# Thirteen expert tiles inside the mixer steps: a fused Mamba mixer and mixture-of-experts layer on one core

## The chip, the cores and the metric

The kernel runs on one core of one Trainium2 chip. The metric is device microseconds of one launch. Before the change the median of three runs is 4983.12 us (4978.73 to 4983.15).

## The reference, cut to what matters

All tensors are float32. There are 4096 tokens (8 sequences of 512) of width 512.

```
x  = x + mamba(layernorm(x))        # in_proj 512 -> 2*1024, causal conv of 4 taps, silu,
                                    # x_proj 1024 -> 128 + 16 + 16, dt_proj 128 -> 1024,
                                    # softplus, scan over time with 16 states per channel,
                                    # y * silu(z), out_proj 1024 -> 512
x  = x + moe(layernorm(x))          # 8 experts, top 2 of 8, weights renormalised
# one expert on its rows:  (silu(r @ w1[e]) * (r @ w3[e])) @ w2[e]     512 -> 1792 -> 512
```

The scan is `h = h * exp(delta*A) + delta*x*B_t` and `y_t = sum_n h*C_t`. The experts see the rows of layernorm(x) after the mixer; each token's row goes to two experts, and each expert's result, times its routing weight, is added to the output.

## The kernel before, in words

There are two programs in one launch, one after the other.

**The mixer** (`mixer`) works off 256 tokens (T) in each of 16 steps (STEPS). The emission of step s holds three strands at once: the scan of tokens s (`scan`), the front of tokens s+1 (`front`: transposes, x and z products, convolution, dt, softplus), and the back of tokens s-1 (`back`: output product, residual, second norm, routing, scattering rows to the expert buffer `rows_d`). A step is cut into 16 slots (SLOTS, index u) and each slot into two pieces (32 pieces; a piece is 4 states of one chunk of 128 channels). The order on every engine is written out by hand: `beside(u)` on TensorE and ScalarE and `beside(u, g)` on VectorE say what is done beside the scan in slot u. Per piece

- ScalarE computes four decays `dA` (L468, `decays`), which is allowed once piece k-3 has been scanned;
- VectorE multiplies the inflow `pU` (L869) and scans `hs` (L886), which waits for the decay and for `summed` of piece k-4 (there are NB = 4 buffers);
- GpSimd multiplies `hs` by C (L399, `weigh`) and, in pieces 1 to 12, does one convolution sum (L422);
- TensorE sums over the states by transposes that accumulate (L747, `sums`).

Beside them TensorE does the x products in slots 0 to 3 and the z products in slots 13 to 15 and in slot 0 of the next step (all L624), the output product in slots 3 to 6 (L671), the x_proj products in slots 9 and 10 (L681, L686), the dt products in slots 11 and 12 (L706), the transposes and router logits in slots 10 and 11 (L715, L694), ranks in slot 14 (L724). VectorE adds the residual in slots 5 and 7 (L904, `residual`), after which the second norm and `route` follow in small operations. At the end of a step VectorE does the softplus (L986, L992, L995) and GpSimd issues four indirect DMAs that scatter the rows (L383, `scatter`).

SyncE issues all other DMAs in one fixed order: four loads of `win` of 1 MB a step (L289), `xb`, `xf`, the store of the output rows, and at the end of the step the four broadcast loads of B and C into `bc` (L338, 1 MB each), each held until its old contents have been used. `each_step` unrolls steps -1, 0 and the last four and runs the rest in a hardware loop of 6 turns with 2 steps in each.

**The expert program** (`experts`) starts when the mixer has ended. VectorE works out how many 128-row tiles each expert has; then each tile t takes its rows, transposes them (L1279), makes up and gate products (L1292, 112 products of 128 columns), silu (L1250), and the down product (L1301, 14 products of 512 columns), and GpSimd adds the rows to the output by an indirect DMA (L1165). The weights of one expert are resident and are loaded only where the expert changes. With these inputs there are 67 tiles.

Of the kernel before, what the change touches and what calls it, by code (L numbers as in the profile page):

```python
# [19 lines left out]
F32 = mybir.dt.float32  # L20
# [5 lines left out]
P = 128  # L26
# [26 lines left out]
NT = 2 * TOKENS // P + E - 1  # L53
NT_SURE = 2 * TOKENS // P
# [4 lines left out]
MK = M // P  # L59
LN1P_SMALL = 1.0 / 128  # L60
# [12 lines left out]
def mixer(nc, x, w_in, conv_w, w_x, w_dt, dt_bias, a_log, d_par, w_out, gate, out, rows_d, bc_d, cnt_d):  # L73
    with ExitStack() as ctx:
# [8 lines left out]
        win = [sb(f"win{s}", [P, DC, 4 * P]) for s in range(2)]  # L83
# [13 lines left out]
        xb = sb("xb", [P, TT, D])  # L97
        rows = [sb(f"rows{k}", [P, TT, RW]) for k in range(2)]
# [16 lines left out]
        x2T = sb("x2T", [P, DC, T])  # L115
# [25 lines left out]
        pM = [pb(f"pM{s}", [P, 2, T]) for s in range(2)]  # L141
# [20 lines left out]
        pT = pS[:, :].rearrange("p (d q) -> p d q", d=DC)  # L162
        pR = pS[:, 0:2 * (TT + 1) * E].rearrange("p (a t e) -> p a t e", a=2, t=TT + 1)
# [13 lines left out]
        win_in = [sem(f"win_in{s}") for s in range(2)]  # L177
# [48 lines left out]
        second_rows = sem("second_rows")  # L226
# [11 lines left out]

        pool_turn = sem("pool_turn")
# [4 lines left out]
        NSET = 12 + NB  # L244
# [7 lines left out]
        def each_step(eng, emit):  # L252


            for s in (-1, 0):
                emit(s, s % 2)
            with eng.Fori(0, (STEPS - 4) // 2) as i:
                emit(2 * i + 1, 1)
                emit(2 * i + 2, 0)
            for s in range(STEPS - 3, STEPS + 1):  # L260
                emit(s, s % 2)
# [3 lines left out]
        def has(s):  # L265

            if not isinstance(s, int):
                return True, True, True, True
            return 0 <= s < STEPS, s + 1 < STEPS, s + 2 < STEPS, s >= 1

# [3 lines left out]
        def _(sp):  # L274
# [9 lines left out]
            def step(s, odd):  # L284
                scan, front, ln1, back = has(s)
                f, r = s + 1, s - 1

                def load_win(j):
                    sp.dma_start(win[j % 2][:, :, :], w_in[:, :, j * 4 * P:(j + 1) * 4 * P]).then_inc(win_in[j % 2], 16)  # L289

                def load_weights():
# [5 lines left out]
                    sp.dma_start(out[TOKENS:TOKENS + P, :], x2T[:, 0:D // T, :]).then_inc(weights_in, 16)  # L297

                if front:

                    hold(z_mm, PAIRS * s + 2)
                    load_win(0)
                if back:
                    hold(x1_stored, 16 * r)
                    hold(xn2, TT * r)
                    sp.dma_start(xb[:, :, :], tokens(x, r)).then_inc(xb_in, 16)
                if front:
                    hold(z_mm, PAIRS * s + 4)
                    load_win(1)
                if isinstance(s, int) and s < 0:  # L310
                    load_weights()
                if ln1:
# [3 lines left out]
                if front:  # L316
                    hold(x_mm, PAIRS * f + 2)
                    load_win(2)
                    hold(x_mm, PAIRS * f + 4)
                    load_win(3)  # L320
                if back:
                    hold(x1_ready, TT * r + TT)
                    sp.dma_start(tokens(out, r), xb[:, :, :]).then_inc(x1_stored, 16)
                if front:
# [4 lines left out]
                    sp.dma_start(bc_d, bcs[:, :]).then_inc(bc_stored, 16)  # L329
                    hold(bc_stored, 16 * f + 16)  # L330
# [15 lines left out]
            sp.dma_start(cnt_d, ebase[0:1, :]).then_inc(cnt_stored, 16)  # L346
            sp.wait_ge(cnt_stored, 16)
# [5 lines left out]
        def _(pool):  # L353
            pool.memset(x2T[:, 0:D // T, :], 0.0).then_inc(consts_set, 1)
# [5 lines left out]
            for i, v in enumerate((LN1P_SHIFT, LN1P_SMALL, EPS)):  # L360
# [14 lines left out]
                      allow_small_or_imprecise_dtypes=True).then_inc(consts_set, 1)  # L375
            def scatter(n, k, t):
# [1062 lines left out]
```

## Time and profile before

| | |
|---|---|
| median of 3 runs | 4983.12 us |
| time of the profiled execution | 4978.98 us |
| span of its trace, first to last instruction | 4977.2 us |
| mean granted TensorE clock | 0.917 |
| busy: PE, DVE, ACT, POOL | 4293.8, 2425.1, 1883.4, 1703.3 us |

The span and the profiled execution's time are 1.8 us apart, so sums made on the trace can be set against the times directly. PE is TensorE, PEld its weight load, DVE VectorE, ACT ScalarE, POOL GpSimd, SP SyncE. A float32 product shows as two instructions. The busy time of PE counts time at either clock, so that the same work shows as more busy time where the clock was low.

### The profile page before, as it was taken

What the parts mean: (1) busy time and instruction counts of PE and PEld (TensorE: products, weight loads), DVE (VectorE), ACT (ScalarE), POOL (GpSimd) and SP (SyncE); (2) the same over time, 40 slices, a digit from 0 to 9 for tenths busy, and PEclk for the clock granted to TensorE, in tenths of its full rate; (3) what the DMA queues carried; (4) which work ended last, traced back from release to release, by engine and by line L of the source; (5) the groups of instructions that cost most, each with busy time, mean ns of one, the idle gap of its engine ahead of it and who ended that gap; (6) DMA issues with size and microseconds to landing.
All of it is one profiled execution on the core that took longest, in us unless ns stands there. A gap on an engine that the chain in (4) does not pass through costs nothing.

```text
span 4977.2 us, 73101 instructions
## 1 busy us (share of the span) xinstructions
PE 4293.8 (86%) x25764; PEld 3442.3 (69%) x25764; DVE 2425.1 (49%) x3184; ACT 1883.4 (38%) x3876; POOL 1703.3 (34%) x1215
## 2 busy tenths in 40 slices
PE   6677777777777777775599999999999999999999
PEld 4556555655656566554488888888878878878877
DVE  3999999999999999999200000000000000000000
ACT  6777777777777777765000000000000000000000
POOL 3667676666767667675100000000000000000000
PEclk8888888888888888886799999999999999999999
DMA  3121122222112222210300303003031030120300
GB/s 141 71 70 55 68 90 90 85 82 74 53 67 90 90 85 81 77 60 17 133 15 15 101 14 104 13 13 105 13 101 17 13 101 17 51 63 17 101 13 15
DMA packets 132824, 308.67 MB, mean 62 GB/s; under 512 B 8596, under 2 KB 17428, under 8 KB 124308
## 3 DMA queue, kind: packets, MB, share of 16 engines
q1 hardware_dynamic: 116564, 269.55, 15.6%
q0 software_dynamic: 14768, 34.41, 3.7%
q10 hardware_dynamic: 1296, 2.37, 0.1%
q8 instruction: 89, 1.46, 0.1%
q14 instruction: 107, 0.88, 0.1%
HBM read 920.96 MB, written 45.95 MB: 194 GB/s over the span
## 4 chain that ended last, share of the span: by engine, by line
PE 51%; ACTq 0%; DMA 0%; issue 0%; POOL 0%; DVE 0%; ACT 0%; SPq 0%; POOLq 0%; DVEq 0%
PE pA L1292 17%; PE pB L1292 17%; PE pD L1301 16%; PE pX L1279 1%; DMA rows_d<-pad 0%; ACTq L1260 0%; ACTq L1261 0%; DMA xr<-rows_d 0%; POOL out L1165 0%; ACTq L1259 0%; POOL tnum L1153 0%; DVE ow L1386 0%; ACT xT L1263 0%; POOL pad L1146 0%; SPq L1182 0%
## 5 line engine op out<-in xcount | busy, mean ns | idle before, releaser
L399 POOL TENSOR_TENSOR hs<-hs,bc 128x1024 f32<-128x1024 f32 x512 | 1213.1, 2369 | 404.1 <-DVE hs L886 382.7
L886 DVE TENSOR_TENSOR_SCAN hs<-dA,pU 128x1024 f32<-128x1024 f32 x512 | 1168.5, 2282 | 22.9 <-DVE pU L869 2.1
L747 PE MATMUL pY<-ident,hs 128*128 128x128 f32 x4096 | 647.2, 314 | 464.4 <-POOL hs L399 464.3
L1250 ACT ACTIVATE gate<-pA 128x512 f32<-128x512 f32 (+1 forms) x268 | 145.7, 544 | 2311.1 <-PE pB L1292 2311.1
L1292 PE MATMUL pA<-xT,w1s 128*128 128x128 f32 x7504 | 992.7, 275 | 0.7 <-ACT xT L1263 0.7
L1292 PE MATMUL pB<-xT,w3s 128*128 128x128 f32 x7504 | 992.0, 275 | 0.0
L747 PEld LDWEIGHTS pY<-ident,hs 128*128 128x128 f32 x4096 | 543.6, 162 | 587.1 <-POOL hs L399 510.7
L1292 PEld LDWEIGHTS pA<-xT,w1s 128*128 128x128 f32 x7504 | 920.0, 192 | 32.7 <-issue 31.6
L1165 POOL DMA_INDIRECT out<-ow,trow x67 | 104.6, 1561 | 2437.7 <-DVE ow L1386 2401.0
L1292 PEld LDWEIGHTS pB<-xT,w3s 128*128 128x128 f32 x7504 | 914.2, 192 | 0.0
L468 ACT ACTIVATE dA<-delta,aneg 128x255 f32<-128x255 f32 x2048 | 849.5, 507 | 149.9 <-DVE hs L886 136.0
L1301 PE MATMUL pD<-w2s,hT 128*128 128x512 f32 x1876 | 816.2, 592 | 0.0
L1382 DVE TENSOR_TENSOR hT<-gate,pB 128x512 f32<-128x512 f32 (+1 forms) x268 | 166.5, 621 | 1111.9 <-ACT gate L1250 1111.6
L869 DVE TENSOR_TENSOR pU<-pZ,bc 128x1024 f32<-128x1024 f32 x512 | 629.5, 1230 | 29.6
L1301 PEld LDWEIGHTS pD<-w2s,hT 128*128 128x128 f32 x1876 | 351.2, 190 | 416.6 <-issue 416.6
L624 PE MATMUL pM<-xnT,win 128*128 128x256 f32 x2048 | 518.9, 413 | 4.9 <-ACT uv L531 3.1
L624 PEld LDWEIGHTS pM<-xnT,win 128*128 128x128 f32 x2048 | 427.8, 214 | 70.3 <-ACT uv L531 3.5
L1386 DVE TENSOR_SCALAR ow<-pD,wrow 128x512 f32<-128x512 f32 x67 | 50.3, 751 | 784.7 <-PE pD L1301 784.7
L671 PE MATMUL pS<-wout,sz 128*128 128x512 f32 x512 | 249.2, 633 | 1.4 <-issue 0.9
L422 POOL TENSOR_TENSOR xc<-xc,uv 128x512 f32<-128x512 f32 x192 | 227.0, 1182 | 13.3 <-POOL uv L416 6.1
L1377 DVE CAST trow<-xr 128x1 int32<-128x1 f32 x67 | 10.3, 154 | 405.4 <-DMA out<-ow,trow 388.0
L671 PEld LDWEIGHTS pS<-wout,sz 128*128 128x128 f32 x512 | 102.6, 209 | 107.6 <-issue 106.0
(168 smaller groups left out, 2568.4 us busy)
## 6 DMA issues: line engine op xcount, KB each, us to landing
w1s<-in_w SPq DMA_DIRECT2D x204, 1024.0 KB
w3s<-in_w SPq DMA_DIRECT2D x204, 1024.0 KB
w2s<-in_w SPq DMA_DIRECT2D x204, 1024.0 KB
win<-in_w_in SPq DMA_DIRECT2D x64, 1024.0 KB, 5.3
bc<-bc_d SPq DMA_DIRECT2D x64, 1024.0 KB, 4.8
w1s<-in_w SPq DMA_DIRECT2D x68, 512.0 KB
w3s<-in_w SPq DMA_DIRECT2D x68, 512.0 KB
w2s<-in_w SPq DMA_DIRECT2D x68, 512.0 KB
```

Of the source, the lines that this page charges most:

```text
L399: pool.tensor_tensor(hs[b][:, :, :], hs[b][:, :, :], bc[:, N + g * PN:N + (g + 1) * PN, :], ALU.mult)\
L422: pool.tensor_tensor(xcf[:, 2 * pair:2 * pair + 2, :], xcf[:, 2 * pair:2 * pair + 2, :], y[:, 2 * k:2 * k + 2, k:k + T], ALU.add).then_inc ...
L468: e = act.activation(dA[k % NB][:, i, 1:T], delta[:, c, 1:T], ACT.Exp, scale=aneg[:, c, n:n + 1])
L624: m = pe.matmul(ps[:, h, :], win[j % 2][:, d, wcol:wcol + P], rowsT[:, d, :], start=d == 0, stop=d == DC - 1)
L671: m = pe.matmul(pO[:, :], szr[:, c, t * P:(t + 1) * P], wout[:, c, :], start=c == 0, stop=c == CH - 1)
L747: m = pe.matmul(pY[c % 2][:, t * P:(t + 1) * P], hs[k % NB][:, i, t * P:(t + 1) * P], ident[:, :], start=g == 0 and i == 0 and t == 0, sto ...
L869: dve.tensor_tensor(pU[:, :, :], pDx[:, :].rearrange("p (a t) -> p a t", a=1).to_broadcast([P, PN, T]), bc[:, g * PN:(g + 1) * PN, :], ALU ...
L886: dve.tensor_tensor_scan(hs[b][:, :, :].rearrange("p n t -> p (n t)"), dA[b][:, :, :].rearrange("p n t -> p (n t)"), pU[:, :, :].rearrange ...
L1250: act.activation(gate[q % 2][:, 0:n, :], pA[q % 2][:, 0:n, :], ACT.Silu).then_inc(silu, 1)
L1292: m = pe.matmul(ps[q % 2][:, k, :], ws[:, d, cols], xT[:, d, :], start=d == 0, stop=d == DC - 1)
L1301: m = pe.matmul(pO[:, :], hT[:, k, :], w2s[:, k, :], start=k == 0, stop=k == MK - 1)
L1382: dve.tensor_tensor(hT[:, lo:lo + n, :], gate[q % 2][:, 0:n, :], pB[q % 2][:, 0:n, :], ALU.mult)\
```

## The change: what it does, and the diff

One full tile of 128 rows of one expert is worked off in each of the mixer steps 3 to 15 (13 tiles). At the end of the step before, VectorE picks the expert with the most rows not yet worked off (`pick`, 8 operations on one partition). In the step SyncE loads the rows, and the expert's 11 MB of weights through a ring of three buffers `ew` of 512 KB, in 21 loads. TensorE transposes the rows in slot 2, makes 16 products of 128 columns in each of slots 4 to 10 and the 14 down products of 512 columns in slots 11 to 15, all into one PSUM bank `pE`. ScalarE takes tanh(g/2) of each up round, VectorE makes `(tanh + 1) * g` and `* 0.5 * up` from it. In the next step, after piece 2, GpSimd adds the rows to the output. The expert program takes 13 tiles fewer and starts at each expert's next row. To make room for `pE` the two banks `pM0` and `pM1` become one, with the x products alternating between it and `pS`, and the z and dt products all in `pM`; `win` becomes three buffers of 512 KB. The rows to be scattered are normalised in place in `xb`, so the second set waits until the first has been written. `each_step` unrolls steps -1 to 3 and the last three, and loops 5 times over 2 steps.

```diff
-NT = 2 * TOKENS // P + E - 1
-NT_SURE = 2 * TOKENS // P
+EARLY0 = -(-(E * (P - 1) + 1) // (2 * T)) + 1      # 3
+EARLY = STEPS - EARLY0                              # 13
+NT_SURE = 2 * TOKENS // P - EARLY
+NT = NT_SURE + E - 1
+PK = 2
+ROUNDS = MK // PK                                   # 7
+EW = 3
+EWLOADS = 3 * ROUNDS                                # 21
-        win = [sb(f"win{s}", [P, DC, 4 * P]) for s in range(2)]
+        win = [sb(f"win{s}", [P, DC, 2 * P]) for s in range(3)]
+        ew = [sb(f"ew{i}", [P, 2 * D]) for i in range(EW)]
-        pM = [pb(f"pM{s}", [P, 2, T]) for s in range(2)]
+        pM = pb("pM", [P, 2, T])
+        pE = pb("pE", [P, 512])
+        pX = [pS[:, :].rearrange("p (h t) -> p h t", h=2), pM]
+        UP0, DOWN = 4, {11: (0, 4), 12: (4, 8), 13: (8, 10), 14: (10, 12), 15: (12, 14)}
# SyncE, order within one step
+                if tile:
+                    hold(e_next, jt + 1)
+                    expert = sp.value_load(epick_i[0:1, 0:1], min_val=0, max_val=E - 1)
+                    row = sp.value_load(epick_i[0:1, 1:2], min_val=0, max_val=DUMMY - P)
+                    for i in range(EW):
+                        load_expert(i)          # each held until load i-3 has been used
...
+                if tile:
+                    hold(ew_used, EWLOADS * jt + 2 * ROUNDS)      # xf comes after up round 7
+                    sp.dma_start(xf[:, :, :], tokens(x, s + 2)).then_inc(xf_in, 16)
...
+                    hold(z_mm, PAIRS * f + 3)
+                    load_win(0, 1)
+                if front:
                     hold(bc_stored, 16 * f + 16)
                     for g in range(UPC):                          # the four bc loads
# GpSimd
+                if k == 1 and t == 0:
+                    ge(pool, scattered, 16 * TT * (2 * n + 1))
+                    pool.tensor_copy(xb[:, :, WCOL], w_second[:, :]).then_inc(second_w, 1)
+                    if i == 2 and early(s)[1]:
+                        add_rows(s - 1 - EARLY0, s - 1)
# ScalarE
+                def read_dt(q):
+                    ge(act, dt_mm, 4 * f + q + 1)
+                    for h in range(2):
+                        ...                     # Abs and Identity of pM[:, h, :]
+                    if tile and UP0 <= u < UP0 + ROUNDS:
+                        ge(act, ew_used, EWLOADS * jt + 2 * (u - UP0) + 2)
+                        ge(act, e_h, ROUNDS * jt + u - UP0)
+                        act.activation(eth[:, :, :], pEup[:, 0, :, :], ACT.Tanh, scale=0.5).then_inc(e_tanh, 1)
# TensorE
+                def expert(u):
+                    if UP0 <= u < UP0 + ROUNDS:
+                        j = u - UP0
+                        ge(pe, e_h, ROUNDS * jt + j)
+                        for w in range(2):
+                            i = 2 * j + w
+                            ge(pe, ew_in[i % EW], 16 * (EWLOADS // EW * jt + i // EW + 1))
+                            for k in range(PK):
+                                for d in range(DC):
+                                    m = pe.matmul(pEup[:, w, k, :], part[:, d, k * P:(k + 1) * P], exT[:, d, :], ...)
+                            m.then_inc(ew_used, 1)
+                    if u in DOWN:
+                        for k in range(*DOWN[u]):
+                            m = pe.matmul(pE[:, :], ehT[:, k, :], ew[i % EW][:, k % PK * D:(k % PK + 1) * D], ...)
# VectorE, slot u, after the first scan of the slot (g == 1)
+                    j = u - UP0 - 1
+                    if 0 <= j < ROUNDS and g == 1:
+                        ge(dve, e_tanh, ROUNDS * jt + j + 1)
+                        dve.scalar_tensor_tensor(eth, eth, 1.0, pEup[:, 0], ALU.add, ALU.mult).then_inc(e_half, 1)
+                        ge(dve, e_half, ROUNDS * jt + j + 1)
+                        dve.scalar_tensor_tensor(ehT[:, PK * j:PK * (j + 1), :], eth, 0.5, pEup[:, 1],
+                                                 ALU.mult, ALU.mult).then_inc(e_h, 1)
```

## Rows read from the trace of the kernel before

**Rows 1.** The page: busy time and share of the span, then tenths in 40 slices

```profile
PE 4293.8 (86%) x25764; PEld 3442.3 (69%) x25764; DVE 2425.1 (49%) x3184; ACT 1883.4 (38%) x3876; POOL 1703.3 (34%) x1215
...
PE   6677777777777777775599999999999999999999
...
DVE  3999999999999999999200000000000000000000
...
PEclk8888888888888888886799999999999999999999
```

**Rows 2.** Windows of mixer and expert program: start:end, length, busy by engine, clock

```profile
400.00:2220.00 1820.00, 1383.33 (x6773) 1068.97 (x6772) 1719.52 (x2102) 1324.19 (x2771) 1257.19 (x891) 0.85 0.21 74
2640.00:4900.00 2260.00, 2260.00 (x15443) 1856.00 (x15442) 208.03 (x424) 166.86 (x301) 95.13 (x61) 1.00 0.18 48
```

**Rows 3.** Chain that ended last, 2790 to 2870 us: start, length, what

```profile
2794.85 0.89 PE pB L1292 x8
...
2819.41 12.02 PE pD L1301 x28
...
2856.88 12.02 PE pD L1301 x28
```

**Rows 4.** Line 593, once a step: count, duration in ns, first and last start

```profile
L593 ACT ACTIVATE delta<-uv,ones x16: 2002/2005/2012, 78.8 to 2228.2; 128x2048 f32<-128x2048 f32 x16
```

**Rows 5.** Groups of VectorE, 400 to 2220 us: busy, mean ns, idle before

```profile
L886 DVE TENSOR_TENSOR_SCAN hs<-dA,pU 128x1024 f32<-128x1024 f32 x406 | 926.5, 2282 | 17.4 <-DVE pU L869 1.9 <-DVE pU L876 1.8
...
L986 DVE SCALAR_TENSOR_TENSOR uv<-dA,uv 128x1024 f32<-128x1024 f32 x24 | 50.1, 2124 | 0.0
L897 DVE TENSOR_TENSOR sz<-pY,sz 128x256 f32<-128x256 f32 x102 | 42.7, 418 | 0.1
...
L904 DVE TENSOR_TENSOR xb<-pS,xb 128x512 f32<-128x512 f32 x26 | 18.0, 691 | 23.9 <-PE pS L671 23.9
...
L848 DVE TENSOR_TENSOR head<-delta,aneg 128x128 f32<-128x128 f32 x6 | 1.8, 292 | 22.6 <-issue 22.6
```

**Rows 6.** Timeline of VectorE, one step: start, length, operation, idle before

```profile
934.35 2.29 DVE L886 TENSOR_TENSOR_SCAN hs<-dA,pU 128x1024 f32<-128x1024 f32 x1
...
946.63 1.23 DVE L869 TENSOR_TENSOR pU<-pZ,bc 128x1024 f32<-128x1024 f32 x1
...
989.39 0.69 DVE L904 TENSOR_TENSOR xb<-pS,xb 128x512 f32<-128x512 f32 x1 [2.10 <-PE pS L671]
```

**Rows 7.** Timeline of TensorE, 930 to 1045 us

```profile
934.77 2.32 PE L624 MATMUL pM<-xnT,win 128*128 128x256 f32 x10
...
980.50 3.60 PE L671 MATMUL pS<-wout,sz 128*128 128x512 f32 x8
983.93 1.91 PE L747 MATMUL pY<-ident,hs 128*128 128x128 f32 x16
...
1012.49 1.97 PE L747 MATMUL pY<-ident,hs 128*128 128x128 f32 x8 [2.96 <-POOL hs L399]
```

**Rows 8.** Timeline of GpSimd at the start of that step

```profile
949.97 0.96 POOL L383 DMA_INDIRECT rows_d<-rows,idx  x1 [0.30 <-issue]
950.93 0.20 POOL L396 COPY state<-hs 128x4 f32<-128x4 f32 x1
```

**Rows 9.** Timeline of SyncE's queue, then DMA issues: count, KB each, us to landing

```profile
925.46 14.03 SPq L336 DMA_DIRECT2D bc<-bc_d  x4
...
win<-in_w_in SPq DMA_DIRECT2D x49, 1024.0 KB, 5.3
bc<-bc_d SPq DMA_DIRECT2D x49, 1024.0 KB, 4.7
...
out<-ow,trow POOLq DMA_INDIRECT x61, 4.8
```

**Rows 10.** Groups of ScalarE, 400 to 2220 us: two of its table loads, one tap copy

```profile
L505 ACT ACTIVATE uv<-pM,convw 128x256 f32<-128x256 f32 x294 | 117.8, 483 | 0.0
...
L593 ACT ACT_TABLE_LOAD x12 | 15.4, 1283 | 0.2
L600 ACT ACT_TABLE_LOAD x12 | 15.4, 1283 | 0.2
```

More of the change, by code:

```diff
@@ L96, in mixer @@
         xf = sb("xf", [P, TT, D])
-        xb = sb("xb", [P, TT, D])
-        rows = [sb(f"rows{k}", [P, TT, RW]) for k in range(2)]
+        xb = sb("xb", [P, TT, RW])
         xnT = [sb(f"xnT{s}", [P, DC, T]) for s in range(2)]
@@ L176, in mixer @@
         xn1 = sem("xn1")
-        win_in = [sem(f"win_in{s}") for s in range(2)]
+        win_in = [sem(f"win_in{s}") for s in range(3)]
         turned1 = sem("turned1")
@@ L237, in mixer @@
         tok_set = sem("tok_set")
+        e_next = sem("e_next")
+        e_step = sem("e_step")
+        e_rows = sem("e_rows")
+        e_meta = sem("e_meta")
+        ew_in = [sem(f"ew_in{i}") for i in range(EW)]
+        ew_used = sem("ew_used")
+        e_turned = sem("e_turned")
+        e_xT = sem("e_xT")
+        e_tanh = sem("e_tanh")
+        e_half = sem("e_half")
+        e_h = sem("e_h")
+        e_tok = sem("e_tok")
+        e_ow = sem("e_ow")
+        e_added = sem("e_added")
         pool_turn = sem("pool_turn")
@@ L285, in step, with load_win @@
                 scan, front, ln1, back = has(s)
+                tile = early(s)[0]
                 f, r = s + 1, s - 1
-                def load_win(j):
-                    sp.dma_start(win[j % 2][:, :, :], w_in[:, :, j * 4 * P:(j + 1) * 4 * P]).then_inc(win_in[j % 2], 16)
+                jt = s - EARLY0
+                def load_win(z, pair):
+                    slot, col = (WIN_Z if z else WIN_X)[pair], (PAIRS * z + pair) * 2 * P
+                    sp.dma_start(win[slot][:, :, :], w_in[:, :, col:col + 2 * P]).then_inc(win_in[slot], 16)
                 def load_weights():
@@ L314, in step @@
+                if back:
+                    hold(scattered, 16 * 2 * TT * r)
+                    hold(x1_stored, 16 * r)
+                    sp.dma_start(xb[:, :, 0:D], tokens(x, r)).then_inc(xb_in, 16)
+                if front:
+                    hold(x_mm, PAIRS * f + 3)
+                    load_win(1, 3)
+                    hold(x_mm, PAIRS * f + 4)
+                    load_win(1, 1)
+                if ln1 and not tile:
                     hold(turned1, TT * f + TT)
                     sp.dma_start(xf[:, :, :], tokens(x, s + 2)).then_inc(xf_in, 16)
[L316 to L320, printed above, removed]
+                if tile:
+                    for i in range(EW, 9):
+                        load_expert(i)
@@ L321, in step @@
                 if back:
                     hold(x1_ready, TT * r + TT)
-                    sp.dma_start(tokens(out, r), xb[:, :, :]).then_inc(x1_stored, 16)
+                    sp.dma_start(tokens(out, r), xb[:, :, 0:D]).then_inc(x1_stored, 16)
+                if tile:
+                    for i in range(9, 14):
+                        load_expert(i)
                 if front:
@@ L436, in _ @@
             pool.wait_ge(scattered, 16 * 2 * TT * STEPS)
+            pool.wait_ge(e_added, 16 * EARLY)
         @block.scalar
@@ L572, in step @@
                         decays(u + 1)
+                    else:
+                        halfway(u)
                     if u < SLOTS - 1:
@@ L618, in step, with dt @@
                 f, r = s + 1, s - 1
+                tile, jt = early(s)[0], s - EARLY0
                 xcf, szr = xc[1 - odd], sz[1 - odd]
-                def project(ps, rowsT, wcol, j, h):
+                def dt(q):
+                    if q == 0:
+                        ge(pe, dtr_copied, f + 1)
+                    else:
+                        ge(pe, dt_read, 4 * f + q)
+                    for h in range(2):
+                        c = 2 * q + h
+                        m = pe.matmul(pM[:, h, :], wdt[:, c * P:(c + 1) * P], dtr[:, :], start=True, stop=True)
+                    m.then_inc(dt_mm, 1)
@@ L697, in beside @@
                     if u in (11, 12) and front:
[L698 to L707 removed]
+                        dt(2 * (u - 11))
                     if u == 10 and back:
@@ L718, in beside @@
                         z_pair(u - 13, f, xnT[1 - odd])
+                    if tile:
+                        expert(u)
                     if u == 14 and back:
@@ L835, in step @@
                 f, r, fodd = s + 1, s - 1, 1 - odd
+                (tile, _, picks), jt = early(s), s - EARLY0
                 xcs, xcf = xc[odd], xc[1 - odd]
@@ L1001, in beside @@
                     c = u // UPC
+                    if tile:
+                        expert(u, g)
                     if scan and u % UPC == 0 and c >= 2 and g == 0:
```

335 lines of the change are left out of this document (243 added, 92 removed).

## The prediction

> **What bounds the kernel now.** I read the page first. Its slices show two programs end to end [rows 1]: in the first 18 or so VectorE is at nine tenths and TensorE at seven, in the last 20 TensorE is at nine and all else is near nothing. The windows give the sizes [rows 2]. From 2640 to 4900 us TensorE is busy for 2260 of 2260 us at a granted clock of 1.00, so the expert program is TensorE's alone. From 400 to 2220 us VectorE is busy 1719.5 of 1820 us (94%), ScalarE 73%, GpSimd 69%, TensorE 1383.3 us (76%) at a mean clock of 0.85.
>
> The chain of waits gives the price of a tile: the 28 down instructions start at 2819.41 and again at 2856.88, so 37.47 us, of which 12.02 are the down products and the rest up products of 0.89 us per 8 instructions [rows 3]. The Ln of the softplus (L593) runs once a step, 16 times from 78.8 to 2228.2 us: a step lasts 2149.4 / 15 = 143.3 us [rows 4].
>
> Why a step lasts 143 us: the scan (2.28 us) runs 32 times, and almost nothing else ends VectorE's idle time. The named waits in the 1820 us are 23.9 us for TensorE's output product (L904) and 22.6 us of "issue" before L848, the first operation of the loop body, 4.5 us at each of five back edges [rows 5]. So VectorE sets the mixer, TensorE the experts, and each has the other engine partly free.
>
> **The change part by part, against the profiled span of 4977 us (4979 us for that execution, 4 us under the median of 4983).**
>
> *Removed.* 13 tiles of the expert program: 13 x 37.47 = 487 us. All of it is on the path, since TensorE never rests there. Nothing is late in its place: the rows and weights of a tile come in beside it as before.
>
> *Added, TensorE.* A tile in the mixer is the same products, at full clock the same 37.5 us. Room for it: 1383.3 us in 1820 is 108.9 us per step at a clock of 0.85, which is 92.6 us of work at full clock, an estimate. Eight transposes after a rest of 2.96 us take 1.97 us, sixteen without a rest 1.91 us [rows 7]: the first at the level of 1.2 GHz, the second at 2.4. With fewer rests most of the step should run at 2.4 GHz. 92.6 + 37.5 = 130 us then stand in a step of 143. It fits on average, with about 10 us lost at each boundary between steps where TensorE waits for VectorE and ScalarE; it doesn't fit in every slot.
>
> *Added, VectorE, direct.* Two scalar_tensor_tensor of 128x256 in each of 7 rounds, reading PSUM and SBUF. The nearest row is L897, same form, 0.42 us [rows 5]; back to back its pitch is a little less, and the second waits for the first: 0.80 us a round, 5.6 us a step. Bounds: 0.33 x 2 x 7 = 4.6 us (pitch alone), and a quarter of L986 (2.12 us for 1024 columns [rows 5]), 0.53 x 2 x 7 = 7.4 us. Eight picks and one copy of the token number at 0.1 to 0.15 us: 1.1 us. Sum **6.7 us** a step, all of it on VectorE's path.
>
> *Added, waits of VectorE for TensorE in slots 4 to 7.* A round is TensorE, then tanh, then VectorE in the next slot after its first scan. TensorE's slot 4 holds 3.6 us of output product, 1.9 of sums, 0.7 of turning y, [rows 7] and now 3.6 us of up products: 9.7 us, against a VectorE slot of two pieces of 3.7 us plus a feed and the new 0.8, about 8.9. Slots 5 and 6 are alike; 7 and 8 have nothing else and catch up. VectorE waits for TensorE there already (2.10 us before the residual [rows 6]). Behind the waiting round on VectorE stands the next scan. I take 5 us a step; nothing if TensorE's better clock pays for it, and at most 3 x 3.6 + 2.1 = 13 us.
>
> GpSimd belongs to the same sum. The second pair of scatters now waits until the first pair has landed; the nearest landing is 4.8 us for an indirect store [rows 9]. GpSimd goes straight from its last scatter at 949.97 to the first piece at 950.93 [rows 8], so its pieces start some 5 us later, plus about 1.5 us for the added row store after piece 2. It has 3.95 us of work per piece while it convolves, against VectorE's 3.8, so the delay isn't won back before slot 6, and the sums and the output product come later. The four buffers (15 us) cover the scan, not the residual: 2 of the 5 us are this. In the three steps without a tile it costs 2 us each, **6 us** in all.
>
> *Added, slots 10 and 11.* TensorE has the dtr product (3.6 us), two transposes with ScalarE between them, and the up round: about 11 us. VectorE meets that tanh after its first scan in slot 11. The dt products now go through one bank in four quarters, each behind ScalarE's reading of the one before. I take 2.5 us; from 0 to 7 us (each of three more exchanges with ScalarE at 2 us of reading).
>
> *Added, the end of the step.* The four bc loads move on SyncE behind the wait for the z product of slot 15 and behind a win load. Before, the first was issued at 925.46 [rows 9]; that z product (10 instructions at the start of the window shown) ends at 937.1 [rows 7]. Issue at about 938.5, one 512 KB load ahead (half of 5.3 us), 4.7 us to landing [rows 9]: 945.8, and VectorE's next pU stands at 946.63 [rows 6]. A cover of 20 us shrinks to 1. Whenever TensorE is late in slot 15, the scan is late too: 1.8 us; from 0 to 8 us (four loads of 4.7 us against 10 us of softplus).
>
> *Hidden.* The 21 weight loads: a load is issued when the buffer three back has been used, about a slot (9 us) before its use, and half of win's 5.3 us is 2.7 us. Bounds 0 and, at the full 5.3 us each, still 0. The late xf load (after up round 7, needed in slot 13) has more than a slot. ScalarE: seven tanh at about the 0.48 us of L505 [rows 10], two copies, less one copy of the rows: +3.5 us in an engine that rests for a quarter; nothing.
>
> The Trainium skill ("ScalarE: Activation LUTs", section "Table sets: the hidden batching unit") puts tanh with exp in one set, which would spare the loads; but it also says that ln then exp need one load, and the trace has one before each (L593 and L600, 1.28 us [rows 10]). By it tanh is free, and my sum agrees; since its other line isn't borne out here, the case where it fails stands below with a chance.
>
> The skill ("DMA: Bandwidth & Descriptors", section "Bandwidth") also wants 1 MiB or more per DMA for three quarters of peak, and the change halves that size. No row here shows 1 KB runs; if it doubled the transfer time, 5.3 us would still be under a slot and the sum would stay.
>
> *The ends.* The last scatter is on the path into the expert program: +5 us. One back edge fewer, 4 instead of 5: -4.5 us.
>
> **Sum.** A tile step grows by 6.7 + 5 + 2.5 + 1.8 = 16 us; 13 x 16 = 208. 4979 - 487 + 208 + 6 + 5 - 4.5 = 4706.5. I say **4705 us**. In general the time is 4498.5 + 13 g for a growth of g us per tile step; the change breaks even at g = 37.
>
> **The rivals.**
>
> A. *VectorE's own operations are all that shows*: g between 6.7 and 12, say 8, **4602 us**. For it: 13 us of room on TensorE, and a better clock. Against it: VectorE already waits for the output product, and the tight slots lie together.
>
> B. *TensorE becomes the bound.* The clock doesn't rise, since waits on tanh and on the products of VectorE make new rests in each round: 108.9 + 37.5/0.85 = 153 us, plus 10 us at the boundary, is 163: g = 20. With the bc loads late as well (5 us), g = 25: **4823 us**. For it: rests under 3 us already leave the clock at the lower level [rows 7]. Against it: nine slots will have hardly a rest.
>
> C. *Tanh and exp don't share a table.* Two loads of 1.28 us in each of 7 rounds are 18 us more on ScalarE in a step of which it rests 38; half exposed, g = 25, **4823 us**; bounds 4705 and 4705 + 13 x 18 = 4939.
>
> D. *Slower.* The round is a ring of three engines: TensorE can't start round j+1 before VectorE's product of round j, VectorE waits for tanh, and the sums that free the scan's buffers are queued on TensorE behind the products. If TensorE's work isn't beside the scan at all but between two scans, all 37.5 us and the 6.7 of VectorE stand in the step: g = 44, 4498.5 + 13 x 44.2 = **5073 us**. It decides from g = 37, when more than 30 of the 37.5 us are exposed. For it: the scan may run only four pieces ahead. Against it: four pieces are 15 us, more than any one slot adds.
>
> **How the numbers follow.** Forecast (g from 12 to 20: 4655 to 4759) 0.50; A 0.18 (4586 to 4655); B 0.22 (4759 to 4860); C 0.05; D 0.04; something that undoes nearly all the gain to within 0.2%, which is about what a measurement of this kernel tells from no change, 0.01. The range takes the forecast, most of A and the nearer half of B: **4615 to 4810 us**. Faster 0.95, same 0.01, slower 0.04.
>
> **What would show it.** The chain still goes through L1292 and L1301's lines, with 54 tiles of 37.47 us. The Ln of the softplus should come every 159 us in the tile steps and every 145 in the others. The granted clock of the mixer rises to 0.93 or more. VectorE's idle time names the tanh and the residual at 3 to 8 us a step, most of it in slots 5 to 7 and 11, and pU at the start of a step waits for bc by 1 to 3 us. No table load before tanh (a third group of loads beside it would be C). If tile steps stay under 155 us, the waits were overrated; above 163 us with a clock under 0.9 it is B; if TensorE waits for `ew`, the cover that I gave the ring was wrong.

## The result, and the profile after

The changed kernel takes 4790.66 us (median of 4 runs, 4779.15 to 4794.46) against 4981.69 us of the kernel before in the same comparison: ratio 0.9613, 95% interval 0.9601 to 0.9625. It is 191 us faster. The forecast was 4705 us, 277 us faster; the range of 4615 to 4810 us holds the time. The profiled execution took 4794.05 us, its span 4792.3 us.

The page, the same lines as [rows 1]:

```profile
PE 4208.5 (88%) x25764; PEld 3403.0 (71%) x25764; DVE 2471.3 (52%) x3377; ACT 1872.3 (39%) x3912; POOL 1706.9 (36%) x1233
...
PE   5777888888887988888887499999999999999999
...
DVE  3999988888888888888889300000000000000000
...
PEclk8788989989999989999898699999999999999999
```

VectorE has fallen from nine tenths to eight in the slices of the tile steps, although it has more to do; TensorE and its clock have risen. The expert program has 54 tiles. Its chain (the same view as [rows 3]) still shows down products 37.46 us apart:

```profile
2820.61 12.02 PE pD L1565 x28
...
2858.07 12.02 PE pD L1565 x28
```

So the 487 us taken away are as forecast; the span is 184.9 us shorter (4977.2 to 4792.3), so the mixer and its end gave back 302. The Ln of the softplus (now L752) places them. From its fourth start to its last there are 12 steps, in the trace before from 495.2 to 2228.2 us, now from 505.9 to 2513.6: 144.4 us became 167.3. The view of L752, as [rows 4]:

```profile
L752 ACT ACTIVATE delta<-uv,ones x16: 2002/2006/2010, 83.7 to 2513.6; 128x2048 f32<-128x2048 f32 x16
```

12 x 22.9 = 275 us. The other 27 us are 10.7 before that fourth start and 16.6 behind the last one, where the thirteenth tile stands in a step without a front.

A window of tile steps, the same view as [rows 2] (start:end, length, busy of PE, PEld, DVE, ACT, POOL, then clock, share of the DMA engines, GB/s):

```profile
500.00:2500.00 2000.00, 1673.13 (x9485) 1346.66 (x9484) 1719.64 (x2270) 1289.21 (x2733) 1213.70 (x861) 0.92 0.42 136
```

Per step of 167.3 us VectorE is busy 143.9 us and idle 23.5; per step of 144.4 us it was busy 136.4 and idle 8.0. Of 22.9 us of growth 7.4 are operations and 15.5 are waits. VectorE's waits in the 2000 us, which hold 12 steps (engine, line, releaser: us in total, times, longest):

```profile
DVE eth L1213 <- ACT eth L713: 84.7, 47, 5.5
...
DVE y L988 <- ACT sd L679: 35.3, 12, 3.4
DVE xb L1107 <- PE pS L877: 33.3, 12, 4.2
DVE pZ L1145 <- ACT le L701: 30.8, 12, 4.1
DVE pZ L1046 <- issue: 26.2, 4, 6.7
...
DVE pZ L1167 <- PE pS L924: 14.8, 11, 1.7
...
DVE hs L1089 <- ACT dA L629: 7.7, 8, 3.2
```

The tanh takes 7.1 us a step. The residual has gone from 1.9 (23.9 us in 12.6 steps, [rows 5]) to 2.8. The square root of the second norm (2.9), the router's exp (2.6) and the ranks (1.2) are new: VectorE hardly ever waited for them in the windows before.

How one step comes by these waits is seen on three timelines (start, length, operation, idle before). VectorE:

```profile
1403.04 0.69 DVE L1107 TENSOR_TENSOR xb<-pS,xb 128x512 f32<-128x512 f32 x1 [3.85 <-PE pS L877]
...
1438.54 0.17 DVE L988 RECIPROCAL y<-sd 128x2 f32<-128x2 f32 x1 [3.35 <-ACT sd L679]
...
1456.92 0.42 DVE L1213 SCALAR_TENSOR_TENSOR eth<-eth,pE 128x256 f32<-128x256 f32 x1 [2.51 <-ACT eth L713]
...
1468.95 0.42 DVE L1213 SCALAR_TENSOR_TENSOR eth<-eth,pE 128x256 f32<-128x256 f32 x1 [3.92 <-ACT eth L713]
```

ScalarE:

```profile
1424.85 0.39 ACT L713 ACTIVATE eth<-pE 128x256 f32<-128x256 f32 x1 [5.19 <-PE pE L810]
...
1430.11 1.91 ACT L671 ACTIVATE xc<-xc 128x2048 f32<-128x2048 f32 x1
...
1433.61 3.29 ACT L629 ACTIVATE dA<-delta,aneg 128x255 f32<-128x255 f32 x8
...
1438.22 0.29 ACT L679 ACTIVATE sd<-mv,series 128x2 f32<-128x2 f32 x1
```

TensorE:

```profile
1448.24 4.37 PE L887 MATMUL pM<-xc,wx 128*32 128x256 f32 x16
1452.55 3.84 PE L810 MATMUL pE<-xf,ew 128*128 128x128 f32 x32
...
1457.97 3.62 PE L893 MATMUL pM<-xc,wx 128*128 128x256 f32 x16
```

ScalarE stands 5.19 us for the up products before a tanh. Decays, the silu of the convolution with a table load on each side of it (L671), and the next decays are queued behind that tanh and ahead of the square root, which therefore starts only at 1438.22; VectorE, in slot 8, waits 3.35 us for it. In slot 9 TensorE does the B and C product first (4.37 us) and only then the up products, and VectorE waits 2.51 us for their tanh. In slot 10 the dt-rank product (3.62 us) and two transposes stand ahead of the up products, and the wait is 3.92 us. Added up by slot over the 12 steps, the tanh waits are 16.8 us in slots 5 to 7, nothing in 8 and 9, 18.1 in slot 10 and 49.8 in slot 11.

The wait for the router's exp comes about otherwise. The same step on TensorE, ScalarE and VectorE:

```profile
1481.33 3.60 PE L819 MATMUL pE<-ew,ehT 128*128 128x512 f32 x8
...
1486.76 0.47 ACT L603 ACTIVATE uv<-pM,dtb 128x256 f32<-128x256 f32 x1 [1.84 <-PE pM L789]
...
1488.36 1.91 ACT L698 ACTIVATE uv<-uv 128x2048 f32<-128x2048 f32 x1
...
1490.40 0.18 DVE L1145 TENSOR_REDUCE pZ<-le 128x2 f32<-128x16 f32 x1 [3.02 <-ACT le L701]
```

Four down products (L819) stand ahead of the last quarter of the dt product. ScalarE waits for that quarter, then takes the softplus's exp over 2048 columns (L698), and the router's small exp is queued behind it.

TensorE has time enough in the step as a whole (busy 140.0 us of 167.3); what VectorE stands for is the place of the work in TensorE's and ScalarE's queues.

### The profile page after: what moved, and what is told of

The parts are those of the page before. It is cut to its first block and busy times, and to the rows that moved or that the text cites. A ratio compares the mean times of both kernels' runs of the same rounds, so it can differ in the third digit from the quotient of the medians.

```text
span 4792.3 us, 73789 instructions
## 1 busy us (share of the span) xinstructions
PE 4208.5 (88%) x25764; PEld 3403.0 (71%) x25764; DVE 2471.3 (52%) x3377; ACT 1872.3 (39%) x3912; POOL 1706.9 (36%) x1233
## 3 DMA queue, kind: packets, MB, share of 16 engines
q1 hardware_dynamic: 273078, 412.71, 26.2%
## 5 line engine op out<-in xcount | busy, mean ns | idle before, releaser
L1514 ACT ACTIVATE gate<-pA 128x512 f32<-128x512 f32 x216 | 117.4, 544 | 1861.0 <-PE pB L1556 1861.0
L1556 PE MATMUL pA<-xT,w1s 128*128 128x128 f32 x6048 | 800.6, 275 | 0.7 <-ACT xT L1527 0.7
L1556 PE MATMUL pB<-xT,w3s 128*128 128x128 f32 x6048 | 799.9, 275 | 0.0
L1556 PEld LDWEIGHTS pA<-xT,w1s 128*128 128x128 f32 x6048 | 741.8, 192 | 26.4 <-issue 25.3
L1556 PEld LDWEIGHTS pB<-xT,w3s 128*128 128x128 f32 x6048 | 737.3, 192 | 0.0
L1565 PE MATMUL pD<-w2s,hT 128*128 128x512 f32 x1512 | 657.8, 592 | 0.0
L1072 DVE TENSOR_TENSOR pU<-pZ,bc 128x1024 f32<-128x1024 f32 x512 | 629.0, 1228 | 22.6
L1647 DVE TENSOR_TENSOR hT<-gate,pB 128x512 f32<-128x512 f32 x216 | 134.1, 621 | 898.8 <-ACT gate L1514 898.7
L827 PE MATMUL pM<-xnT,win 128*128 128x256 f32 x1536 | 404.4, 423 | 3.0 <-ACT uv L604 1.7
L810 PEld LDWEIGHTS pE<-xf,ew 128*128 128x128 f32 x2912 | 350.7, 199 | 45.7 <-issue 23.6
L810 PE MATMUL pE<-xf,ew 128*128 128x128 f32 x2912 | 357.6, 283 | 18.8 <-DVE ehT L1218 18.6
```

The source lines that it names most:

```text
L810: m = pe.matmul(pEup[:, w, k, :], part[:, d, k * P:(k + 1) * P], exT[:, d, :], start=d == 0, stop=d == DC - 1)
L827: m = pe.matmul(ps[:, h, :], w[:, d, h * P:(h + 1) * P], rowsT[:, d, :], start=d == 0, stop=d == DC - 1)
L1072: dve.tensor_tensor(pU[:, :, :], pDx[:, :].rearrange("p (a t) -> p a t", a=1).to_broadcast([P, PN, T]), bc[:, g * PN:(g + 1) * PN, :], ALU ...
L1556: m = pe.matmul(ps[q % 2][:, k, :], ws[:, d, cols], xT[:, d, :], start=d == 0, stop=d == DC - 1)
L1565: m = pe.matmul(pO[:, :], hT[:, k, :], w2s[:, k, :], start=k == 0, stop=k == MK - 1)
L1647: dve.tensor_tensor(hT[:, lo:lo + n, :], gate[q % 2][:, 0:n, :], pB[q % 2][:, 0:n, :], ALU.mult)\
```

## Experiments

Each ratio is against the kernel before, run on the same chip beside it (4981 to 4983 us).

**1. The rearrangement alone.** No tile in the mixer.

```diff
-EARLY = STEPS - EARLY0
+EARLY = 0
...
-            return EARLY0 <= s < STEPS, EARLY0 <= s - 1 < STEPS, EARLY0 <= s + 1 < STEPS
+            return False, False, False
-            sp.wait_ge(e_next, EARLY)
-            pool.wait_ge(e_added, 16 * EARLY)
```

> All of the rearrangement (one dt and z bank, three smaller win buffers, the scatter in two halves, the bc loads behind the z product, the later unrolling), but no tile in the mixer: all 67 tiles stay in the expert program. Theory W (the growth of a tile step comes from the tile itself, from waits between TensorE, ScalarE and VectorE): the three steps without a tile grew by 1.9 us each between the traces, so 16 steps give +30 us, less one loop jump of 5 us: about 5007 us, and a step of 145.5 us. Rival R (the rearrangement is what costs, each step 6 us or more): 5075 us or more. If it comes out at 4980 the rearrangement is free and my 6 us for it were too much.

Measured: 5021.03 us, ratio 1.0078 (1.0061 to 1.0094); 146.8 us a step. The rearrangement costs 40 us, 2.4 us a step, more than theory W's 30 and far less than R. Its VectorE waits from 840 to 2180 us:

```profile
DVE xb L1103 <- PE pS L873: 23.7, 13, 3.9
DVE pZ L1042 <- issue: 16.4, 4, 4.3
DVE hs L1085 <- ACT dA L625: 13.2, 9, 2.2
```

The scan's wait for decays was absent before and is 1.4 us a step here. It stands near the x products, not at the dt quarters: eight of the nine come 40 to 46 us behind the Ln. Before the decays of one of them ScalarE had waited for an x product in the one bank:

```profile
982.73 0.47 ACT L660 ACTIVATE xc<-pM,convw 128x256 f32<-128x256 f32 x1 [4.83 <-PE pM L823]
```

In this window ScalarE waits 66.3 us in all for x products in that bank; before the change it waited 32.0 us for x products (L503) in the same window. Whether the one bank is what makes them late wasn't tried. A tile costs 167.3 - 146.8 = 20.5 us on top.

**2. Fewer up products.** Only a quarter of the inputs is multiplied, so 28 products in place of 112; everything else stays.

```diff
-                                for d in range(DC):
-                                    m = pe.matmul(pEup[:, w, k, :], part[:, d, ...], exT[:, d, :],
-                                                  start=d == 0, stop=d == DC - 1)
+                                m = pe.matmul(pEup[:, w, k, :], part[:, 0, ...], exT[:, 0, :], start=True, stop=True)
```

> Leaves out three of four up products of each mixer tile (only the first 128 of the 512 inputs are used), so TensorE has 28 products in place of 112 per tile, 18.7 us less per tile step; loads, tanh, VectorE's products and all waits stay. Theory W1 (TensorE's time stands in VectorE's way through the tanh): the waits of 7.1 (tanh), 2.8 (residual), 2.9 (square root) and 2.6 us (exp of the router) per tile step go nearly all, so 10 to 15 us of the 24 go: 4791 - 13 x 13 = about 4620 us. Rival W2 (the chain of hand-overs costs, not TensorE's time): 4740 to 4790 us.

Measured: 4674.85 us, 0.9382 (0.9366 to 0.9398); 157.5 us a step. That is between W1 (4620) and W2 (4740 to 4790), somewhat nearer W1. 18.7 us less of TensorE bring 9.8 us a step by the traces and 8.9 by the medians. Of VectorE's waits from 500 to 2350 us (11.7 steps) these two matter:

```profile
DVE pZ L1144 <- ACT le L701: 29.8, 11, 3.0
...
DVE eth L1212 <- ACT eth L713: 7.2, 9, 1.2
```

The tanh wait has fallen from 7.1 to 0.6 us a step and the square root's is gone. The router's exp still costs 2.5 us: it isn't the up products that hold it, which agrees with the timeline above.

**3. VectorE's products later.** The products of a round come one scan later; the down products move too, since the last round is ready later.

```diff
-                    if 0 <= j < ROUNDS and g == 1:
+                    if 0 <= j < ROUNDS and g == 3:
-        UP0, DOWN = 4, {11: (0, 4), 12: (4, 8), 13: (8, 10), 14: (10, 12), 15: (12, 14)}
+        UP0, DOWN = 4, {12: (0, 4), 13: (4, 8), 14: (8, 10), 15: (10, 14)}
```

> VectorE makes the two products of a round after the second scan of the slot instead of the first (3.7 us later), and the down products stand in slots 12 to 15 (4, 4, 2, 4) instead of 11 to 15, so that the last product need not be there in slot 11. Theory W1: the tanh is then ready when VectorE comes, the wait of 7.1 us per tile step goes and little comes back, since TensorE's next round isn't due before: 4791 - 13 x 6 = about 4713 us. Rival W3 (TensorE is the bound in these slots, so that VectorE's wait only moves to the residual, the square root or the scan's buffers): 4770 to 4800 us.

Measured: 4861.99 us, 0.9761 (0.9745 to 0.9777); 172.0 us a step. My expectation fell, and beyond the rival too: 71 us slower than the changed kernel. VectorE's waits from 500 to 2350 us, then one tanh on ScalarE and the square root that VectorE waits for behind it:

```profile
DVE y L988 <- ACT sd L679: 80.7, 11, 8.5
DVE eth L1213 <- ACT eth L713: 51.1, 18, 5.2
```

```profile
1286.48 0.39 ACT L713 ACTIVATE eth<-pE 128x256 f32<-128x256 f32 x1 [3.42 <-PE pE L810]
...
1293.11 0.17 DVE L988 RECIPROCAL y<-sd 128x2 f32<-128x2 f32 x1 [8.00 <-ACT sd L679]
```

The tanh wait went down to 4.8 us a step (10.8 steps), but the square root's rose from 2.9 to 7.5. TensorE may not start a round before VectorE's product of the last one. With that product later the round and its tanh are later (ScalarE waits 3.42 us here), and the decays and the square root are queued behind the tanh. The ring is closed: what one engine gives up, another waits for.

**4. The second scatter pair later.**

```diff
                 for i in range(PIECES):
                     if scan:
                         weigh(s, odd, i)
+                    if i == 0 and (not isinstance(s, int) or s >= 2):
+                        for t in range(TT):
+                            scatter(s - 2, 1, t)
...
-                    for k in range(2):
+                    for k in range(2 if isinstance(s, int) and s == STEPS else 1):
```

> The second pair of scatters is issued after the first piece of the next step, so GpSimd doesn't stand for the first pair to land (80.4 us in 12 steps, 6.7 us a step). Theory P (GpSimd's late start is part of the residual wait and of the later waits): GpSimd starts its first piece 3 to 5 us earlier, the residual wait of 2.8 us goes, 2 to 3 us a step in 16 steps: about 4750 us. Rival: the four buffers cover the delay and nothing changes, 4785 to 4795 us. If the issue of two scatters between the first pieces is worse than the wait, it is slower: 4810 us.

Measured: 4788.9 us, 0.9611 (0.9595 to 0.9627): no change. GpSimd's wait for the first pair (80.4 us in 12 steps of the changed kernel) is gone from the trace, VectorE's waits are about as before (residual 2.7 and tanh 7.3 us a step), and the time is the same.

**5. Small weight loads.** The first tile's loads are whole, all later ones 8 KB, so the later tiles multiply by old weights.

```diff
+                    if not (isinstance(s, int) and s == EARLY0):
+                        sp.dma_start(ew[i % EW][:, 0:16], w1[bass.ds(expert * D, P), 0:16]).then_inc(ew_in[i % EW], 16)
-                    if i < 2 * ROUNDS:
+                    elif i < 2 * ROUNDS:
```

> After the first mixer tile each of the 21 weight loads moves 8 KB (16 columns of one chunk) instead of 512 KB, so the tiles work on old weights; all instructions and waits stay. In the trace of the changed kernel the bc loads land after 12.3 us (4.7 before) and the first scatters after 7.4 us. Theory W (engines wait for each other, not for transfers): 4785 to 4795 us, as the changed kernel. Rival M (the 10 MB a step crowd the other transfers, and that is part of the growth): 3 us or more per tile step, 4750 us or less.

Measured: 4780.44 us, 0.9598 (0.9582 to 0.9614), overlapping the changed kernel's interval. The DMA issues of both, first the changed kernel (count, KB, us to landing):

```profile
ew<-in_w SPq DMA_DIRECT2D x250, 512.0 KB, 4.4
bc<-bc_d SPq DMA_DIRECT2D x48, 1024.0 KB, 12.3
```

```profile
bc<-bc_d SPq DMA_DIRECT2D x50, 1024.0 KB, 12.0
...
ew<-in_w SPq DMA_DIRECT2D x231, 8.0 KB, 1.7
```

The bc loads land after 12 us with and without the weights' traffic. The median is 10 us lower and the intervals don't tell that from nothing; theory W holds. What makes the bc loads slow is then most likely that they stand together, which was not tried. SyncE's queue in the changed kernel has the four issues within 1.89 us, where [rows 9] has them spread over 14.03 us and landing after 4.7:

```profile
1342.14 1.89 SPq L455 DMA_DIRECT2D bc<-bc_d  x4
```

**6. No hardware loop.** Same steps, all written out.

```diff
-            with eng.Fori(0, turns) as i:
-                ...
+            for s in range(-1, STEPS + 1):
+                emit(s, s % 2)
```

> All 18 steps written out, no hardware loop. The four loop jumps show 26.2 us of idle VectorE in the changed kernel (22.6 us at five jumps before). If these are all that the loop costs: 4791 - 26 = 4765 us. Rival: straight code has to be fetched too, and the idle time only spreads: 4790 us.

Measured: 4767.65 us, 0.9565 (0.9549 to 0.9581): 23 us faster than with the loop. Nearly all of the 26.2 us of idle time at the four jumps came back. VectorE has no wait for the bc loads in this trace either.

**7. Another order.** TensorE, and the tanh of slots 9 and 10 on ScalarE likewise:

```diff
+                    if tile and u in (5, 9):
+                        expert(u)                    # before the output product and the B, C product
                     if u in OUT_SLOTS and back:
...
+                    if tile and u == 10:
+                        expert(u)                    # before the two transposes
                     if u == 10 and back:
...
-                    if tile:
+                    if tile and u not in (5, 9, 10, 11, 12):
                         expert(u)
...
                     if u in (11, 12) and front:
                         dt(2 * (u - 11) + 1)
+                    if tile and u in (11, 12):
+                        expert(u)
```

> Same work, other order in four places: in slot 5 the up products stand before the output product, in slot 9 before the B and C product, in slot 10 before the two transposes (with tanh moved alike on ScalarE), and in slots 11 and 12 the down products stand behind the second dt quarter. Theory W (VectorE stands for TensorE work queued ahead of what it waits for): the tanh waits of slots 10 and 11 (6.4 of the 7.1 us per tile step) and the wait for the router's exp (2.5 us) go for the most part, 6 to 8 us a tile step: 4791 - 13 x 7 = about 4700 us. Rival W3 (the total of TensorE's work is the bound in the middle of the step and the wait only moves): 4780 to 4800 us, as in the run with the later products, where it moved to the square root.

Measured: 4741.14 us, 0.9515 (0.9499 to 0.9530); 163.7 us a step. Half of the gain that was expected, but better than W3: 3.6 us a step. From 500 to 2350 us (11.3 steps) the router's exp is down from 2.6 to 1.3 us a step and the tanh from 7.1 to 3.7, with nothing left in slot 10; the square root's wait stays at 2.8. New is a wait of 26.1 us, 2.3 a step, for the router's logits, whose transposes now stand behind an up round.

**8. The same, and the reciprocal half a slot later.**

```diff
-                        if at == (8, 1):
+                        if at == (8, 3):
                             ge(dve, sd2, r + 1)
...
-                        if at in ((8, 3), (9, 0), (9, 1)):
+                        if at in ((9, 0), (9, 1), (9, 2)):
```

> The reordering and also the second norm's first reciprocal one half slot later (slot 8 after the second scan, the rest after it), so that VectorE comes later to the square root that ScalarE delays. Theory: the wait of 2.9 us per tile step goes too, 13 x 2.5 = 33 us under the reordering alone: about 4670 us. Rival: VectorE then waits at the next tanh instead: the same as the reordering alone.

Measured: 4688.2 us, 0.9412 (0.9396 to 0.9427); 158.4 us a step. By the medians that is 53 us less than with the order alone, 4.1 us in each of the 13 tile steps, for a wait of 2.8 us. (The steps of the two traces are 5.3 us apart, but the profiled execution of experiment 7 was 11 us above its median and this one 7 us below.) VectorE's waits from 500 to 2350 us:

```profile
DVE eth L1226 <- ACT eth L653: 28.6, 32, 1.2
...
DVE pZ L1133 <- PE pS L910: 26.1, 11, 3.8
DVE xb L1120 <- PE pS L886: 23.0, 12, 4.0
DVE pZ L1158 <- ACT le L710: 14.3, 11, 1.8
```

The square root is gone from the list, the tanh is down to 2.4 us a step (11.7 steps) and the residual from 2.8 to 2.0. The wait in the ring cost more than its own length: the next round had been held with it.

**9. One product instead of two.**

```diff
-                        dve.scalar_tensor_tensor(eth, eth, 1.0, pEup[:, 0], ALU.add, ALU.mult).then_inc(e_half, 1)
-                        ge(dve, e_half, ROUNDS * jt + j + 1)
```

> Leaves out the first of VectorE's two products of a round (its wait for tanh goes to the one that is left), 7 operations of 0.41 us and their hand-over less per tile step, about 3.1 us. Theory D (VectorE's own operations stand in the step at full price): 4791 - 13 x 3.1 = 4751 us. Rival: where VectorE waits for the tanh, residual or square root anyway, a shorter VectorE only waits longer, so less than half comes back: 4775 us or more.

Measured: 4791.16 us, 0.9618 (0.9602 to 0.9634): nothing. Window and waits from 500 to 2350 us:

```profile
500.00:2350.00 1850.00, 1541.94 (x8804) 1238.61 (x8803) 1570.25 (x2059) 1198.59 (x2529) 1121.98 (x784) 0.92 0.42 136
```

```profile
DVE ehT L1215 <- ACT eth L713: 94.6, 54, 4.4
DVE y L988 <- ACT sd L679: 43.6, 11, 4.3
```

VectorE is busy 141.5 us a step (143.9 in the changed kernel) and idle 25.2 (23.5); the tanh wait grew to 8.5 us a step, the square root's to 3.9 (11.1 steps). Theory D fell: 2.4 us a step would be 31 us. In the changed kernel VectorE's own work no longer sets the step.

**10 and 11. More waits moved, without the loop; then also the second scatter pair later.**

```diff
-                        if at == (5, 0):
+                        if at == (5, 1):
                             residual(0)
-                        if at == (11, 3):
+                        if at == (12, 0):
                             route(0)
```

> The reordering with the later reciprocal, all steps written out, and two more of VectorE's waits moved back: the residual of slot 5 behind that slot's first scan, the copy of the router logits from the end of slot 11 to the start of slot 12. Written out alone gave 23 us; the two waits show 2.2 us each per tile step in the trace of the kernel with the later reciprocal. 4688 - 23 - 13 x 3 = about 4626 us. If the waits only move on: 4665 us.

> The same with the second scatter pair after the first piece of the next step. With most other waits gone the late start of GpSimd may show: 1 us a step, 10 to 20 us faster than without; if the buffers cover it here too, the same.

Measured: 4670.91 us, 0.9374 (0.9359 to 0.9390), and 4652.31 us, 0.9338 (0.9322 to 0.9354), with 157.7 and 155.8 us a step. The first fell short of 4626: it gained 17 us where writing out alone had given 23, so nothing is left of the two moved waits' 4 us a step. They went on to others: from 500 to 2350 us the tanh is back at 4.6 us a step and the router's exp at 2.6. The second is the fastest kernel of this study, 331 us under the kernel before. There the later scatter does bring 19 us, though it brought nothing in the changed kernel. Its two largest waits from 500 to 2350 us:

```profile
DVE eth L1223 <- ACT eth L650: 47.1, 23, 5.6
DVE pZ L1155 <- ACT le L707: 30.5, 11, 3.1
```

**12. The rearrangement alone, second scatter pair later.**

> The rearrangement without tiles, and the second scatter pair after the first piece of the next step. The rearrangement cost 40 us. If GpSimd's wait for the first pair is the larger part of it (it delays the residual of slot 5 in a step that has no other waits): 4995 us. If the dt quarters and the shared bank are: 5015 to 5025 us as before.

Measured: 5024.69 us, 1.0081 (1.0064 to 1.0098): the same as experiment 1. GpSimd's wait for the first scatters is gone (60.0 us there, 1.1 here, from 840 to 2180 us) and isn't what the rearrangement costs. The scan's wait for the decays has nearly gone too (13.2 to 0.8), but the residual's grew (23.7 to 32.7) and one for the router's logits came (0.5 to 9.0). The shared bank for the x, z and dt products, the dt quarters, the smaller `win` buffers and the moved bc loads are left; they weren't tried singly, and which of them it is stays open.

## Why the prediction was right in direction and too high in gain

*Removed, 487 us: right.* 13 tiles of 37.46 us.

*Room on TensorE: right.* It was put at 130 us of work at full clock; busy is 140.0 us a step at 0.92, and 140.0 x 0.92 = 129. The clock rose from 0.85 as said, though to 0.92 and not 0.93.

*VectorE's own operations, 6.7 us: right in size* (7.4 measured), *wrong in kind.* They were called "all of it on VectorE's path". Experiment 9 took 2.4 us of them away and got nothing.

*The waits, 5 + 2.5 + 1.8 = 9.3 us: this is where the sum was mis-sized.* Idle time grew by 15.5 us a step, and not where the terms had put it. Slots 4 to 7 were put at 5 us with GpSimd's share; the tanh waits there are 1.4 us a step and the residual's grew by 0.9, so 2.3. Slots 10 and 11 with the dt quarters were put at 2.5 us, 7 at most; the tanh waits there are 5.7 us and the router's exp behind the dt quarters 2.6, so 8.3. The square root's 2.9 us and the ranks' 1.2 have no term. The rest is small: 0.6 for decays, 0.4 for the loop's jump.

Two things were overlooked. The prediction counted what stands ahead of the up round in slot 10 (about 11 us of TensorE's work) but let only 2.5 us of it reach VectorE. And ScalarE was costed at nothing because it "rests for a quarter". Its share wasn't the point: it does its queue in order, so what it stands for (283.3 us in 12 steps before the tanh, TensorE's dt quarters behind the down products) holds small results behind it, the square root and the router's exp, 5.5 us a step together. That the square root is late through the up products is shown by experiment 2, where its wait is gone; that the exp is late through the down products is borne out by experiment 7, where they stand behind the second dt quarter of their slot, and by 3, where slot 11 has none: its wait is 1.3 and 1.2 us a step there. Experiments 7 and 8 together show what order is worth: the same work in another order, with one result asked for later, takes 102 us less.

*GpSimd's late start, 2 of the 5 us: wrong.* The pause is there (6.7 us a step), and experiments 4 and 12 show that taking it away brings nothing; that the four buffers cover it is the likely reason. Only when other waits were gone (experiment 11) did it cost 1 us a step.

*The bc loads, 1.8 us: wrong.* VectorE waits nowhere for them. They are late as said (issued together behind the z product, landed after 12.3 us), but no wait follows from it, with the loop's jump or without (experiment 6); what covers them wasn't tried.

*The rearrangement, 6 us in steps without a tile: too small.* It is 2.4 us a step and 40 us in all (experiment 1); for the tile steps it had no term of its own apart from GpSimd, the dt quarters and the bc loads.

*The weight ring: right.* TensorE's list of waits has none for `ew`, and with nearly all of its bytes taken away at most 10 us come back.

*The loop, -4.5 us: wrong sign*, 26.2 us at four jumps against 22.6 at five.

Sum with measured terms, over the 12 steps: 7.4 + 15.5 = 22.9 instead of 16. So the range holds the time, but 4790.66 us lies outside the forecast's own stretch (4655 to 4759) and in the one that was given to rival B with a chance of 0.22. That it came no higher is in part luck: the terms that were too high (2.7 us in slots 4 to 7, 1.8 for the bc loads) made up for 4.5 of the 10.9 us that were missing elsewhere.

It is the size of rival B, not its mechanism: B had the clock stay low and TensorE full; the clock rose, TensorE rests 27 us a step, and experiment 8 wins 9 us a step without taking any work away. Rival C is refuted. ScalarE's groups from 500 to 2500 us:

```profile
L629 ACT ACT_TABLE_LOAD x24 | 30.8, 1283 | 0.4
...
L713 ACT ACT_TABLE_LOAD x12 | 15.4, 1283 | 18.0 <-PE pE L810 18.0
```

Of seven tanh a step one has a load, the one that follows the square root; the decays have two a step in its stead, where they had three. Rival D would have needed a growth of 37 us; a tile adds 20.5 us to the rearranged step, a little over half of the 37.5 us that it takes in the expert program.

## What to carry to other kernels

When work is put beside a chain, price the hand-overs and not only the engines' free time: list for each engine, in order, what it will stand for, and then look one instruction behind each such wait, on every engine of the ring. A half-idle engine that must stop in its queue delays everything queued after. Ask late for a result whose use holds up nobody else, and put the producer's work ahead of work that nobody waits for; here order alone brought 102 us on top of the change's 191 (experiment 8). A use that lets another engine start its next round must not be put off: that lost 71 us (experiment 3). And look again after each move, since a wait that is taken out can come back elsewhere in the ring (experiment 10). Shortening the engine with the highest busy share tells whether it is still the bound.

## What the runs showed of the hardware

A VectorE operation on 1x8 numbers took 2.08 us where GpSimd ran beside it, the next one on 1x8 numbers 0.14. From VectorE's timeline and GpSimd's:

```profile
1339.93 2.08 DVE L1188 TENSOR_TENSOR ekey<-ebase,etab 1x8 f32<-1x8 f32 x1
...
1342.07 0.14 DVE L1190 SCALAR_TENSOR_TENSOR ekey<-ekey,etab 1x8 f32<-1x8 f32 x1
```

```profile
1339.63 2.36 POOL L539 TENSOR_TENSOR hs<-hs,bc 128x1024 f32<-128x1024 f32 x1 [2.67 <-DVE hs L1089]
```

It ends at 1342.01, 0.02 us after GpSimd's operation (1339.63 + 2.36). The Trainium skill ("SBUF — State Buffer", section "Who interferes with whom") has a VectorE instruction with two SBUF inputs contend with a GpSimd instruction that reads SBUF, over a shared port pair that it calls an exclusive lock; the trace agrees. In the 12 steps L1188 and L1190 take 1.11 and 1.17 us on the mean: now one meets it, now the other. It cost next to nothing extra: before, the softplus product L986 stood there and took 2.12 us on the mean of two a step [rows 5]; now it takes 1.21 us.

The hardware loop's jump was longer where its body held more: VectorE's idle time there is 4.5 us before L848 [rows 5] and 4.1 us in the rearrangement without tiles, both with 167 VectorE operations a step, and 6.5 us in the changed kernel, with 190.
